# Block 0's first product in four units as the mixed tiles come, and its weight checks moved to the last block

## The reference

```python
def reference(x, fside_BxSxS_0, cond_512, L0_cond_w, L0_cond_u, L0_ffn_W1, L0_ffn_W2):
    mixed = _bi_wkv(x, fside, fside, w, u, cond)
    ...
    # inside _bi_wkv(r, k, v, w, u, time_emb), along the sequence, both ways:
    a = a * decay + exp(k) * v          # numerator
    b = b * decay + exp(k)              # denominator
    out = sigmoid(r) * num / max(den, 1e-8) * (0.8 + 0.2 * tf)
    ...
    h = einsum('bsd,fd->bsf', mixed, W1)
    a = gelu(round(h / 0.1) * 0.1)      # h is clipped to 16 bits after rounding
    return x + einsum('bsf,df->bsd', a, W2)
```

## Time and profile before

| what | value |
|---|---|
| median of three executions | 1751.74 us |
| the profiled execution, its own time | 1751.11 us |
| span in the trace | 1748.8 us |
| mean granted TensorE clock | 0.986 of full |
| busy: PE, DVE, ACT | 1655.3, 1292.6, 933.8 us |
| matmul instructions | 12258 |

### The profile page before, as it was taken

The page is one execution under the profiler, slowest core; times in us unless marked ns, Lnnn a source line. Parts: engine busy times, 40 slices in busy tenths (PEclk is TensorE's granted clock), DMA queues, the critical chain, the costliest instruction groups (busy, mean ns, idle before and its releaser), DMA issues. The chain is left out here.

```text
span 1748.8 us, 30785 instructions
## 1 busy us (share of the span) xinstructions
PE 1655.3 (95%) x12258; PEld 1201.0 (69%) x12258; DVE 1292.6 (74%) x1787; ACT 933.8 (53%) x1450; POOL 24.6 (1%) x44
## 2 busy tenths in 40 slices
PE   1579999899999999999999999999999999999998
PEld 0134444688748886688847887488866888478874
DVE  8977877589697867888787876978778776755222
ACT  3457522574746646385655646467464755455141
POOL 0000020000000000000000000000000000000000
PEclk9789999999999999999999999999999999999999
DMA  9858785768556684757747585676847677465744
GB/s 246 196 159 241 282 298 190 247 195 288 175 211 213 217 268 136 262 183 269 241 142 252 183 271 167 217 233 222 286 137 256 185 251 232 158 206 181 234 135 158
DMA packets 153461, 376.97 MB, mean 216 GB/s; under 512 B 15328, under 2 KB 44256, under 8 KB 152800
## 3 DMA queue, kind: packets, MB, share of 16 engines
q1 hardware_dynamic: 150624, 351.86, 60.6%
q0 software_dynamic: 2688, 23.07, 5.8%
HBM read 347.61 MB, written 67.11 MB: 237 GB/s over the span
## 5 line engine op out<-in xcount | busy, mean ns | idle before, releaser
L754 PE MATMUL ps<-mo,w_ring 128*128 128x256 f16 x6272 | 698.7, 273 | 13.1 <-ACT ps L1098 5.7
L754 PEld LDWEIGHTS ps<-mo,w_ring 128*128 128x128 f16 x6272 | 613.6, 98 | 93.7 <-issue 16.0
L897 PE MATMUL ps<-act,w_ring 128*128 128x512 f16 x1760 | 383.3, 380 | 0.0
L817 PE MATMUL ps<-act,w_ring 128*128 128x256 f16 x3136 | 348.1, 273 | 0.0
L817 PEld LDWEIGHTS ps<-act,w_ring 128*128 128x128 f16 x3136 | 306.0, 98 | 36.3
L897 PEld LDWEIGHTS ps<-act,w_ring 128*128 128x128 f16 x1760 | 172.0, 98 | 203.4
L1654 DVE SCALAR_TENSOR_TENSOR act<-a,act 128x1024 f16<-128x1024 f32 x72 | 88.0, 1222 | 95.9 <-ACT act L1158 95.9
L1183 ACT ACTIVATE q<-tt 128x1024 int8<-128x1024 f32 x64 | 67.2, 1050 | 160.7 <-DMA tt<-in_w_dram 160.7
L1148 ACT ACTIVATE a<-q 128x1024 f32<-128x1024 int16 x128 | 135.3, 1057 | 15.7 <-DVE act L1654 10.7
L1098 ACT ACTIVATE ps<-ps 128x512 f32<-128x512 f32 x70 | 40.7, 581 | 153.3 <-PE ps L754 89.5
L1717 DVE SCALAR_TENSOR_TENSOR tt<-q,tt 128x1024 f32<-128x1024 int8 x64 | 78.1, 1221 | 49.0 <-ACT q L1183 49.0
(11 more groups left out here) (121 smaller groups left out, 1653.4 us busy)
## 6 DMA issues: line engine op xcount, KB each, us to landing
w_ring<-w1s SPq DMA_DIRECT2D x168, 512.0 KB, 4.8
w_ring<-w_half SPq DMA_DIRECT2D x130, 512.0 KB, 5.1
tt<-in_w_dram SPq DMA_DIRECT2D x64, 512.0 KB, 5.3
w_ring<-w2s SPq DMA_DIRECT2D x56, 512.0 KB, 4.9
V<-in_fside_dram SPq DMA_DIRECT2D x64, 256.0 KB, 5.8
R<-in_x_dram SPq DMA_DIRECT2D x64, 256.0 KB, 5.9
w_half<-in_w_dram POOLq DMA_DIRECT2D x16, 1024.0 KB, 8.2
xy<-in_x_dram SPq DMA_DIRECT2D x64, 256.0 KB, 4.9
```

The source lines that it names most:

```text
L754: mm = pe.matmul(dst[:, f, :], wp_ring[:, k, r, f, q, :], mo[:, op, q, p, :], start=(fresh and f == 0 and q == 0 and p == 0), stop=(q == K ...
L817: mm = pe.matmul(dst[:, i, :], wy_ring[:, k, i, 2 * s + j, :], ao[:, s, op, j, p, :], start=(fresh and i == 0 and s == 0 and j == 0 and p ...
L897: mm = pe.matmul(bank[d][:, :], w2_ring[:, k, FPS * (s - SPLIT) + j, :], act[:, act_at(n, s) + j, p, :], start=(s == SPLIT and j == 0 and ...
```

## The change

Block 0's first product is cut in other pieces. Units 0 and 1 take tiles 0 to 3. ACT copies their eight banks to SBUF (`spill01_of`). Units 2 and 3 take tiles 0 to 5 in the same banks. ACT copies these sums out too (`spill23_of`) and writes those of units 0 and 1 back (`reseed01`), bank by bank. Units 0 and 1 take tiles 4 to 7 and are done. Units 2 and 3 take tiles 6 and 7, and DVE adds the copy when it quantises (`quantise23`). Units 4 to 7 are as before. The number of matmuls is the same.

Four weight loads go ahead of tiles 5 and 6 instead of behind tile 7 in SP's list. The second product has four banks instead of two. DVE's order in block 0 is another: the sums of weights and `act_lo` first, block 1's tiles later. The first exponentials of tile 8 stand ahead of the quantising on ACT.

No weight check stands in block 0 and none at the start of block 1. Block n (1 to 6) has the pieces that block n - 1 had, and the last block has 16 of its own beside the two from before, in another buffer but still one at a time.

```diff
--- before.py
+++ after.py
...
-                if at % DT == 0 and at > 0:
-                    sp.wait_ge(s_glo, 4 * quad_unit(at // DT, SPLIT))
-                sp.dma_start(chk_full[:, :], full[at // 4 % STEPS].rearrange("p (i m) -> i p m", i=4)[at % 4]).then_inc(
+                if at == END_CHECKS:
+                    sp.wait_ge(s_mo, 3 * KH * (BLOCKS - 1))
+                elif at % DT == 0 and at < END_CHECKS:
+                    sp.wait_ge(s_glo, 4 * quad_unit(at // DT + 1, SPLIT))
+                sp.dma_start(check_buffers(at)[0], full[at // 4 % STEPS].rearrange("p (i m) -> i p m", i=4)[at % 4]).then_inc(
                     s_chkload, 16)
...
+                if t in (5, 6):
+                    ring_load(2)
                 load_tile(t)
-            for _ in range(4):
-                ring_load()
             load_tile(CT)
             load_tile(CT + 1)
 
...
+                    ring_load(2)
+                    store_sums(s)
+                    if s in (3, 5):
+                        load_tile(g0 + (s + 1) // 2)
+                    if s == 5:
                         residual(0, 0)
                         residual(0, 1)
-                    if s == 6:
-                        load_check(0)
-                    ring_load()
-                store_sums(LAST)
+                load_tile(g0 + 4)
                 ring_load()
-                load_tile(g0 + 5)
                 store_w2sums(0)
-                ring_load(2)
-                load_check(1)
-                ring_load()
-                load_check(2)
+                ring_load(3)
...
+                    if d < 6:
+                        load_tile(g0 + 3 + d)
...
+                    if not nxt:
+                        load_check(at + s - 1)
...
                 ring_load(5)
-                load_check(at)
+                load_check(at if nxt else at + 4)
...
-                load_check(at + 1)
+                load_check(at + 1 if nxt else at + 5)
...
+                else:
+                    load_check(at + 6)
...
-                load_check(at + 2)
+                load_check(at + 2 if nxt else at + 7)
...
+                else:
+                    load_check(at + 8)
                 ring_load(2)
+                if not nxt:
+                    load_check(at + 9)
                 ring_load(4)
+                if not nxt:
+                    load_check(at + 10)
...
+                load_check(at + 3 if nxt else at + 11)
                 ring_load(2)
                 store(n, 0)
                 residual(n, 2)
                 ring_load(2)
                 store(n, 1)
                 residual(n, 3)
-                load_check(at + 4 if nxt else at + 5)
+                load_check(at + 4 if nxt else at + 12)
+                if not nxt:
+                    load_check(at + 13)
...
-                    load_check(at + 6)
+                    load_check(at + 14)
                 store(n, 3)
                 residual(n, 5)
-                load_check(at + 5 if nxt else at + 7)
+                load_check(at + 5 if nxt else at + 15)
...
             def first_hidden():
+
                 slots = [loaded() for _ in range(4)]
-                for t in range(CT):
+
+                def tile_product(s, j, t, first, last):
                     c = tile_of(t)[2]
+                    for p in range(2):
+                        mm = pe.matmul(bank[4 * (s % 2) + j][:, :], w1_ring[:, slots[2 * s + j // 2], j % 2, c, :],
+                                       mix0[:, c, p, :], start=(first and p == 0), stop=(last and p == 1),
+                                       skip_group_check=True)
+                    return mm
+
+                for t in range(KH):
                     pe.wait_ge(s_mix, t + 1)
                     for s in range(2):
                         for j in range(FPS):
-                            for p in range(2):
-                                mm = pe.matmul(bank[4 * s + j][:, :], w1_ring[:, slots[2 * s + j // 2], j % 2, c, :],
-                                               mix0[:, c, p, :], start=(t == 0 and p == 0), stop=(t == CT - 1 and p == 1))
+                            mm = tile_product(s, j, t, t == 0, t == KH - 1)
+                            if t == KH - 1:
+                                mm.then_inc(s_part, 1)
+                slots.extend([loaded() for _ in range(4)])
+                for t in range(CT - 2):
+                    pe.wait_ge(s_mix, t + 1)
+                    for s in (2, 3):
+                        for j in range(FPS):
+                            if t == 0:
+                                pe.wait_ge(s_spill, FPS * (s - 2) + j + 1)
+                            mm = tile_product(s, j, t, t == 0, t == CT - 3)
+                            if t == CT - 3:
+                                mm.then_inc(s_part, 1)
+                for s in range(2):
+                    for j in range(FPS):
+                        pe.wait_ge(s_reseed, FPS * s + j + 1)
+                        for t in range(KH, CT - 2):
+                            tile_product(s, j, t, False, False)
+                for t in (CT - 2, CT - 1):
+                    pe.wait_ge(s_mix, t + 1)
+                    for s in range(2):
+                        for j in range(FPS):
+                            mm = tile_product(s, j, t, False, t == CT - 1)
                             if t == CT - 1:
                                 mm.then_inc(s_h0, 1)
+                for s in (2, 3):
+                    for j in range(FPS):
+                        pe.wait_ge(*quantised0(s - 2, j))
+                        for t in (CT - 2, CT - 1):
+                            mm = tile_product(s, j, t, t == CT - 2, t == CT - 1)
+                        mm.then_inc(s_h0, 1)
...
-                    pe.wait_ge(s_res[0], DT // 2)
+                    pe.wait_ge(s_res[0], DT // 2 - 1)
...
+                if q == 0:
+                    pe.wait_ge(s_res[1], DT // 2)
...
-                k, y = loaded(), d % 2
+                k, y = loaded(), d % 4
                 if h == 0:
-                    pe.wait_ge(s_res[y], d // 2)
-                    if d < 2:
-                        pe.wait_ge(s_q0, FT - FPS)
+                    if d < 4:
+                        pe.wait_ge(*quantised0(LAST - 1, FPS - 1))
+                    else:
+                        pe.wait_ge(s_res[d % 2], d // 2 - 1)
...
+            def spill01_of(b):
+                act_e.wait_ge(s_part, b + 1)
+                sc.activation(spill01[:, b, :], bank[b][:, :], ACT.Copy).then_inc(s_spill, 1)
+
+            def spill23_of(b):
+                act_e.wait_ge(s_part, 2 * FPS + b + 1)
+                sc.activation(spill23[:, b, :], bank[b][:, :], ACT.Copy, scale=1.0 / MIX_SCALE).then_inc(s_spill, 1)
+
+            def reseed01(b):
+                act_e.wait_ge(s_spill, 2 * FPS + b + 1)
+                sc.activation(bank[b][:, :], spill01[:, b, :], ACT.Copy).then_inc(s_reseed, 1)
...
+                if q == 0:
+                    act_e.wait_ge(s_res[0], DT // 2)
...
+                else:
+                    for b in range(2 * FPS):
+                        spill23_of(b)
+                        reseed01(b)
...
+                if t == KH:
+                    for b in range(2 * FPS):
+                        spill01_of(b)
             mix_hi(CT - 1)
+            tile_group(CT)
...
-                for s in range(STEPS):
+                for s in range(2):
+                    for j in range(FPS):
+                        quantise0(s, j)
+                for s in range(4):
+                    for h in range(2):
+                        gelu(0, s, h)
+                        act_hi(0, s, h)
+                for s in range(4, STEPS):
                     quantise0(s, 0)
                     quantise0(s, 1)
+                    if s == 4:
+                        quantise0(s, 2)
+                        quantise0(s, 3)
+                        tile_group_between(g0 + 1)
...
+                    if s == 5:
+                        tile_group_between(g0 + 2)
...
                     quads_hi_11(n, s - 1)
+                    if not nxt:
+                        check_i8(at + s - 2)
...
@@ -1291,41 +1397,39 @@
                 act_hi(n, LAST, 1)
                 if nxt:
                     operands_hi(n + 1, 0)
-                check_i8(at + 2)
+                else:
+                    check_i8(at + 9)
+                check_i8(at + 2 if nxt else at + 10)
...
+                check_i8(at + 3 if nxt else at + 11)
+                check_i8(at + 4 if nxt else at + 12)
...
+                check_i8(at + 5 if nxt else at + 13)
                 if not nxt:
-                    check_i8(at + 6)
-                    check_i8(at + 7)
+                    check_i8(at + 14)
...
+            def quantise23(s):
+
+                for j in range(FPS):
+                    b = FPS * (s - 2) + j
+                    dve.wait_ge(s_h0, FPS * s + j + 1)
+                    dve.wait_ge(s_spill, 2 * FPS + b + 1)
```

(42 more changed lines are left out.)

205 lines of the change are left out of this document (114 added, 91 removed).

## The result

The changed kernel took 1722.26 us (median of four executions, 1721.29 to 1725.35) where the kernel before took 1752.10 (median of four). The ratio is 0.9834, with a 95% interval from 0.9817 to 0.9851, so 26 to 32 us less. The forecast was 1730, with a range of 1721 to 1742: the sign and the place of the gain were right, it was 7 to 8 us too cautious, and the result lies 1.3 us inside the lower end of the range. The profiled execution took 1722.96 us with a span of 1720.6, so 28.2 us less than the one before by either number.

The account below looks back on a forecast made before the run. It took DVE as the bound up to 109 us and TensorE from there. Gains of 30.8 us less losses of 9.9 made 20.9, so 1751.1 became 1730.2 us, with a range of 1721 to 1742.

Parts of the forecast that it names:

- tighter ring loads: Weight loads for units 4 to 6 and in the last block have less time to land: 0.5 us lost, 0 to 4.
- early matmuls: Block 0's first product: 96 matmuls of units 2 and 3 move into TensorE's idle time before 109 us, 20.7 us gained.
- warm start: After block 0's last mixed tile: TensorE comes from nearly unbroken work, so no half clock there, 1.5 us gained.
- banks, second product: Block 0's second product: four output banks give 28 us more room, so the 3.0 us wait for a sum goes.
- block 1's start: Waits of 2.9 us for a residual sum and 2.7 for a seed both go, 5.6 us gained.
- last mixed tile: Block 0: ring loads brought forward delay V of tile 6, with 1.8 us of room assumed; 1.5 us lost.
- end: Last block: a longer chain of single checks delays the last load of x and last sum, 7.9 us lost.
- clock rival: Block 0, 96 to 104 us: clock halves as TensorE goes bank to bank, 6.8 us more, 1737.0; chance 0.08.
- rival of a hidden end: Last block: the chain of checks gets ahead or has shorter links, 7.9 us come back, 1722.3; chance 0.07.
- DVE as the bound: Block 0: the last operand step holds block 1; chances 0.09 partial (1740.5), 0.04 within 0.2%, 0.05 slower.
- That it doesn't do what it says: Block 0: ring slots for units 2 and 3, or copies out and back, come late; some 1735, chance 0.04.
- list of signs at the end of the forecast: Trace signs if right: mixed-tile wait down some 30 us, first product ending near 175, block 1 starting near 287.

Follow-up runs that it names:

- few_early: The changed kernel, but units 2 and 3 take only tiles 0 to 3 early, with tiles 4 and 5 at the end: 1730.81 us, ratio 0.9877.
- best: The changed kernel with two buffers for last-block checks, GpSimd's second-weight copies later and ACT's float16 copy ahead of the next tile's exponentials: 1713.96 us, ratio 0.9783.
- casts_late: The changed kernel with GpSimd's copies of the second weights, but for the first one, behind all those of the first weights: 1721.03 us, ratio 0.9827.
- hi_first: The changed kernel with ACT's float16 copy of tile t - 1 ahead of the exponentials that wait for tile t + 1: 1722.31 us, ratio 0.9829.
- loads_forward: The kernel before with one edit, the four weight loads behind tile 7 moved ahead of tiles 5 and 6, two each: 1752.87 us, ratio 1.0012.
- no_checks0: The kernel before without the first eight weight checks (six in block 0, two at block 1's start), made nowhere: 1741.71 us, ratio 0.9932.
- two_buffers: The changed kernel with the last block's 16 weight checks going through two buffers by turns: 1717.72 us, ratio 0.9806.
- dve_loaded: The changed kernel with 16 extra scans on DVE ahead of block 1's last operands, 20.1 us together: 1738.09 us, ratio 0.9918.

## Why the prediction was right, and where it was off

The gain of 28.2 us in the trace against the forecast's 20.9 splits like this; a minus is a loss. The forecast's tighter ring loads stand as blocks 1 to 6.

| term | forecast | measured | from |
|---|---|---|---|
| early matmuls | 20.7 | 20.7 | few_early: 6.9 for 32, so 0.216 each |
| warm start | 1.5 | 1.5 | 65.7 us from the last mixed tile to the second product, 65.6 forecast |
| banks, second product | 3.0 | 3.3 | 110.5 us instead of 113.8 |
| block 1's start | 5.6 | 9.5 | 2.9 + 6.6 |
| last mixed tile | -1.5 | -3.0 | 112.07 against 109.09 |
| blocks 1 to 6 | -0.5 | 1.0 | within their scatter of 2.8 |
| end | -7.9 | -4.8 | 17.9 against 13.1 from the last output tile on |

*Early matmuls and warm start* were right to a tenth. The copies out hid where the forecast put them, and those out and back ended in time for tile 6. TensorE waited 2.09 us for tile 5 at 95.84, where the forecast had it at work from 87.9 to 91.4 and again from 92.9; the clock was half for some 3 us there (0.54 and 0.61 in the windows from 96 to 100, 1.00 from 100 to 102), which hid in the wait for tile 7. So the clock rival did not decide, and in this kernel it was not put to the test: TensorE came to the banks only about 101 us, when ACT's copies (97.03 to 106.2) were ahead of it, and was never idle between them. In best it met the copies, in the last four banks. Windows on PE of the changed kernel and of best:

```profile
102.00:104.00 2.00, 2.00 (x11) 1.00 0.59 223
```

```profile
100.00:102.00 2.00, 1.78 (x9) 1.00 0.76 173
```

There it idled for about 0.1 us ahead of each bank. Matmuls overlap by 0.38 - 0.216 = 0.16 us, so this is the 0.3 of the rival, and the clock stayed at 1.00; the traces of casts_late and of the kernel both show the same. What lowered the clock in the changed kernel was a wait for a tile, as ahead of the bursts before. The Trainium skill, TensorE: Matmul & The Clock Gate, section "A second HAM failure mode: psum-queue depth-cycling", describes a kernel in which such micro-idles made the clock go up and down; these few didn't.

*The last mixed tile.* The failed step is "the weight made from it ends at 79.0, 1.8 us before DVE needs it". That is the room of one reader of V. ACT works in order, and `mix_hi` of tile 4 stood behind the same wait with 0.07 us of room. hi_first shows it: with the copy ahead, 2.4 of the 3.0 us went, V being just as late. The forecast read the room from the instruction that uses the transfer and not from all that is queued behind it. The half of the loss that loads_forward doesn't have is V of tile 4, issued ahead of the moved loads and used at 54.95, against 53.82 before; in loads_forward and no_checks0 it was used at 53.33 and 54.74, in the others that have it as the changed kernel does at 54.15 to 56.28. Whether that is more than scatter stayed open; in casts_late it was there at 49.79.

*Block 1's start.* Both waits went, as said. The missing 3.9 us are the half clock behind them (3.4) and a wait of 0.5. The forecast had looked at the clock only where tiles come in bursts. no_checks0 also corrects the reason: it has the first 512 matmuls of block 1 done 9.0 us earlier without touching banks or DVE's order. The forecast had seen tile 16's load move up, but not that the checks' loads were what held it and x back.

*Banks.* The term was right, but for the sum of two things: 3.0 taken away, and a new wait of 10.6 that two banks would have had. The forecast named the 28 us of room and not what would use it up.

*The end.* The chain took 1708.92 - 1665.37 = 43.6 us for its six links, where the forecast had 42.7 + 2.4 = 45.1, and its first check stood 37.3 us ahead of the last output tile, as before. The last load of x landed in 3.0 us, not 4.5. That is 1.5 + 1.5 of the 3.1 us. In seven kernels with single checks at the end this stage took 17.9 to 19.9 us, so 4.8 to 6.8 lost: the range of the forecast, 5.1 to 10.3, overlaps with it, and 7.9 was above. The rival of a hidden end falls: two_buffers shows that the end was not hidden and how to hide it.

*DVE as the bound* was refuted with a number: its last operands were ready at 277.5 us, where the forecast said about 275, and dve_loaded gives the room as 9.3 us, set by the last residual sum and not by the operands. *That it doesn't do what it says* didn't happen. The list of signs at the end of the forecast was wrong in several items: the last mixed tile came at 112.07, not at 109 to 111; the last block began 33 us earlier, not 29; the last sum stood 4.8 us behind the output's last matmul, not 8; and TensorE's wait for mixed tiles fell by 15.2 us, not 30. For the 30 I had counted what moves ahead of the last tile and what is saved behind it together; the waits can fall by no more than the work put into them.

## What to carry to other kernels

Work of the bounding engine moved into its idle time is worth its full length, and can be priced to a tenth by a count. The room of a transfer is the least room of all that stands behind its first reader on an in-order engine, so look at the whole queue. When work with loads of its own is moved to a stage with a serial chain, count the links to the end of the kernel and give the chain a second buffer; and price a wait of the matrix engine with the half clock that can follow it.

## What the hardware showed that I had not expected

A wait of about 3 us of TensorE has two prices. In the kernel before, the one of 2.97 us ahead of 227.71 left the clock at 1.00 and the 384 matmuls took 83.0 us; those of 2.92 and 2.72 at block 1 brought it to half. In no_checks0 one of only 2.07 at the first of these places did, and the 384 took 84.7. For a tile of block 0, a wait of 2.09 us at 95.84 in the changed kernel brought it to half, and those of 2.05 in two_buffers and 2.19 in hi_first at the same place left it at 1.00. So a wait of 2 to 3 us costs itself or itself and 1.4 to 1.7 us, and no row here says which. Longer ones cost more: 2.6 us behind 10.6.

The landing time of a transfer of 256 KB in a full stage depends on what other queues carry: V of tile 6 took 9.3 us before, 11.2 in the changed kernel, and at most 5.2 with the same two loads of weights ahead of it but GpSimd's copies of the second weights moved away.
